# Attention 2: the bias of each exponential is made on GpSimd instead of VectorE

## The reference

```python
q = fq_sym((x @ Wq + bq) * scale, axis=-1)      # 16 heads of 16, 1024 queries
k = fq_sym(k, axis=-1);  v = fq_sym(v, axis=2)  # 1024 keys: all rows form one batch
attn = softmax(einsum('bhqd,bhkd->bhqk', q, k))
s = max(attn, axis=-1) / 255                    # fq_unsigned
attn = clip(round(attn / s), 0, 255) * s
out = einsum('bhqk,bhkd->bhqd', attn, v) @ Wp + bp
```

## Time and profile before

| | us |
|---|---|
| median of 3 runs | 1067.88 (1065.49 to 1070.03) |
| the profiled execution | 1065.92 |
| its span (first to last instruction) | 1064.3 |
| first to last start of the 128 exponentials | 315.65 to 511.08 |

### The profile page before, as it was taken

The page is one execution under the profiler, slowest core; times in us unless marked ns, Lnnn a source line. Parts: engine busy times, 40 slices in busy tenths (PEclk is TensorE's granted clock), DMA queues, the critical chain, the costliest instruction groups (busy, mean ns, idle before and its releaser), DMA issues.

```text
span 1064.3 us, 14257 instructions
## 1 busy us (share of the span) xinstructions
PE 720.2 (68%) x4990; PEld 484.0 (45%) x4990; DVE 544.2 (51%) x1256; ACT 387.1 (36%) x676; POOL 324.3 (30%) x338
## 2 busy tenths in 40 slices
PE   5964929930558787878776595294866239999980
PEld 3433514420435554555653484153435237677660
DVE  3995323246779988989344153727796200000002
ACT  3001113301269989999420132232653022202200
POOL 4720730058306766667205002400000320100005
PEclk9985969975668888888868697597898569999995
DMA  5060236638109989899502425430012130531503
GB/s 191 1 217 1 103 103 200 194 73 81 16 1 189 192 169 188 170 195 174 105 1 94 158 80 183 130 100 1 1 45 114 45 133 1 182 118 64 182 25 118
DMA packets 152028, 115.43 MB, mean 108 GB/s; under 512 B 108908, under 2 KB 138766, under 8 KB 150944
## 3 DMA queue, kind: packets, MB, share of 16 engines
q1 hardware_dynamic: 143256, 93.91, 34.2%
q0 software_dynamic: 7104, 19.42, 7.6%
q10 hardware_dynamic: 1608, 1.32, 0.4%
HBM read 63.98 MB, written 25.46 MB: 84 GB/s over the span
## 4 chain that ended last, share of the span: by engine, by line
PE 29%; DVE 9%; POOL 4%; issue 4%; DMA 4%; ACT 2%; POOLq 0%; DVEq 0%
PE psum L2030 8%; PE psum L2021 7%; PE psum L1394 3%; PE psum L187 2%; PE psum L1661 2%; POOL grouped_x_dram L1526 1%; POOL moe_x_dram L431 1%; PE psum L1409 1%; DMA both<-grouped_y_dram,idx 1%; PE psum L1251 1%; POOL both L474 1%; DVE both L1916 1%; DVE both L1913 1%; PE psum L527 1%; DVE stats L142 1%
## 5 line engine op out<-in xcount | busy, mean ns | idle before, releaser
L1200 DVE TENSOR_REDUCE both<-psum 128x1 f32<-128x1024 f32 x128 | 155.8, 1217 | 16.0 <-PE psum L1010 15.3
L929 POOL TENSOR_SCALAR both<-both 128x1024 f16<-128x1024 f32 x128 | 133.7, 1044 | 98.3 <-ACT both L1094 90.5
L1094 ACT ACTIVATE both<-psum,both 128x1024 f32<-128x1024 f32 x128 | 154.2, 1217 | 7.1 <-DVE both L1201 4.4
L431 POOL DMA_INDIRECT moe_x_dram<-xn,moe_idx_to x48 | 48.1, 1002 | 218.9 <-DVE moe_idx_from L419 204.9
L1010 PE MATMUL psum<-both 128*128 128x512 bf16 x256 | 92.6, 451 | 24.8 <-ACT both L1094 21.4
L2058 DVE COPY both<-psum 128x256 f32<-128x256 f32 (+1 forms) x24 | 10.1, 422 | 183.8 <-PE psum L2030 183.8
L2030 PE MATMUL psum<-both 128*128 128x256 f32 (+1 forms) x384 | 85.5, 381 | 0.0
L1031 PEld LDWEIGHTS psum<-both 128*128 128x128 f16 x1024 | 64.0, 100 | 46.9 <-ACT both L1101 14.7
L1031 PE MATMUL psum<-both 128*128 128x16 f16 x1024 | 69.8, 173 | 19.4 <-DVE xn L1208 8.1
L474 POOL DMA_INDIRECT both<-moe_y_dram,moe_idx_from x48 | 50.3, 1047 | 90.4 <-DMA moe_y_dram<-both 76.4
L2030 PEld LDWEIGHTS psum<-both 128*128 128x128 f32 (+1 forms) x384 | 65.2, 172 | 19.9 <-issue 4.2
(11 more groups left out here) (325 smaller groups left out, 1422.7 us busy)
## 6 DMA issues: line engine op xcount, KB each, us to landing
both<-in_l_experts SPq DMA_DIRECT2D x50, 384.0 KB, 3.9
both<-in_l_experts SPq DMA_DIRECT2D x8, 2048.0 KB, 8.8
grouped_y_dram<-both SPq DMA_DIRECT2D x31, 128.0 KB
grouped_x_dram<-zeros SPq DMA_DIRECT2D x15, 256.0 KB, 2.5
moe_x_dram<-zeros SPq DMA_DIRECT2D x1, 2560.0 KB, 9.1
both<-kpad_dram SPq DMA_DIRECT2D x1, 2048.0 KB, 8.1
both<-grouped_x_dram SPq DMA_DIRECT2D x1, 2048.0 KB, 13.1
both<-moe_x_dram SPq DMA_DIRECT2D x2, 1024.0 KB, 6.9
```

The lines of the kernel that those rows point to most:

```text
L431: nc.gpsimd.indirect_dma_start(out=self.x_dram[:, :], out_offset=bass.IndirectOffsetOnAxis(ap=self.idx_to[:, t, k:k + 1], axis=0), in_=xn[ ...
L929: nc.gpsimd.tensor_scalar(r2[n % RSLOTS2], e2[:, n % ESLOTS2, :], 1.0, HALF_BASE, ALU.mult, ALU.add).then_inc(sem("r2_ready"), 1)
L1094: nc.scalar.activation(e2[:, n % ESLOTS2, :], scores_at(n), ACT.Exp, bias=bias2[:, n:n + 1], scale=s2[:, t * H2 + h:t * H2 + h + 1], accum ...
L1200: seq.step(nc.vector.tensor_reduce(nmax2[:, n:n + 1], scores_at(n), AX.X, ALU.max, negate=True))
```

## The change

The bias step leaves DVE. DVE's maximum now signals a semaphore of its own, and POOL makes the bias from it. POOL's order becomes: bias 0, bias 1, rounding 0, bias 2, rounding 1, and so on to the end, so each bias step stands one unit ahead of the rounding of the unit before it.

```diff
         def l1x_rounds_gpsimd(pool):
-            for n in range(H2 * NT):
+            U = H2 * NT
+
+            def exp_bias(n):
+                h, t = n // NT, n % NT
+                pool.wait_ge(sem("nmax2_ready"), n + 1)
+                nc.gpsimd.tensor_scalar(bias2[:, n:n + 1], nmax2[:, n:n + 1], s2[:, t * H2 + h:t * H2 + h + 1], LN255,
+                                        ALU.mult, ALU.add).then_inc(sem("bias2_ready"), 1)
+
+            exp_bias(0)
+            for n in range(U):
+                if n + 1 < U:
+                    exp_bias(n + 1)
                 pool.wait_ge(sem("e2_ready"), n + 1)
                 if n:
                     pool.wait_ge(sem("r2_ready"), n)
@@ l1x_vector
             def top(n):
-                h, t = n // NT, n % NT
                 dve.wait_ge(sem("scores2_done"), n + 1)
-                seq.step(nc.vector.tensor_reduce(nmax2[:, n:n + 1], scores_at(n), AX.X, ALU.max, negate=True))
-                nc.vector.tensor_scalar(bias2[:, n:n + 1], nmax2[:, n:n + 1], s2[:, t * H2 + h:t * H2 + h + 1], LN255,
-                                        ALU.mult, ALU.add).then_inc(sem("bias2_ready"), 1)
+                nc.vector.tensor_reduce(nmax2[:, n:n + 1], scores_at(n), AX.X, ALU.max, negate=True).then_inc(sem("nmax2_ready"), 1)
```

## The result

The changed kernel took 1080.12 us (median of 4 runs, 1076.99 to 1081.90) against 1068.95 for the kernel before: 1.0094 times as long, 95% interval 1.0071 to 1.0117. It is slower by about 10 us (11.2 between the medians). The profiled execution took 1080.09, span 1078.5.

A forecast was written before the change was run, and what follows sets the result against it. In the second attention ACT is nearly full, with 7.1 us lost to DVE's pace and the score ring. 16 cycles at 6.02 and 9 at 6.08 give +3.2, boundaries -0.75: +2.4 us, 1070.3 as median; range 1063.5 to 1079.

The forecast's parts named there:

- rival B: Second attention: the small step on POOL is dear and POOL paces the stage; +9.9 us, 1077.8; chance 0.27.
- d: Last of each cycle's four exponentials a, b, c, d (a behind the copy); forecast to start 3.94 us behind a.
- DVE's pace: Second attention: reduce plus bias step take 1.38 us per unit on DVE; the change cuts this to about 1.25.
- score ring: Ring of three: unit d's scores wait for the end of a's exponential; counted in nine of 25 cycles.
- slow scores: Scores lasting 1.03 us with TensorE at 1.2 GHz; d at 4.00 behind a, nine cycles of 6.08 us.
- The loop through POOL's queue: bias(n+2) queues behind rounding(n), which needs exponential n: c at 2.70, d at 3.94 behind a, cycle 6.02 us.
- the rounding to the next POOL instruction: Link on POOL from a rounding's start to the next instruction's start, taken as 1.03 us.
- B: Duration of the bias step on POOL, taken as 0.22 us, bounds 0.11 and 0.41; counts twice in d's place.
- first link: From the start of exponential a to the start of a's rounding on POOL, taken as 1.41 us.
- The boundaries: Three group boundaries: reciprocal 0.13 us sooner and one gap about 0.12 shorter at each, 3 x -0.25 = -0.75 us.
- Rival C: Late roundings at the group boundaries starve PE: +4.5 us on top of the sum, 1074.8; chance 0.07.
- Rival A: Second attention: POOL is never late, only ACT's pace and the ring bind; -3.9 us, 1064.0; chance 0.13.

The follow-up runs named there:

- e1: Kernel before without any bias step, the exponential taking constant bias and scale columns: 0.9925 times the kernel before.
- e5: Against the changed kernel, POOL makes the bias only for units a and b, DVE for c and d: 0.9959 times the kernel before.
- e7: Against the changed kernel, POOL makes the bias only for units c and d, DVE for a and b: 1.0088 times the kernel before.
- e2: Kernel before, plus a like multiply-add on POOL ahead of each rounding that nobody waits for: 1.0042 times the kernel before.
- e8: Kernel before, plus a two-column add on POOL ahead of each rounding that nobody waits for: cycle 5.992 us against 5.915, one run.
- e4: Changed kernel with POOL's bias step two units ahead of its rounding instead of one: 1.0190 times the kernel before.

## Why the prediction was right in part, and where it was wrong

The measured +0.94%, put on the 1067.88 from which the prediction starts, is 1077.9 and lies in the range of 1063.5 to 1079, but I forecast +2.4 us and no measurable difference, at 0.59. What came is rival B, which I had at 0.27 and priced at +9.9 us; about +11 was measured in the medians and +12.0 in the stage. That the range held is luck in part: its upper end had d at 4.32 and cycles of 6.40, just what was measured (4.31, 6.40), but from a bias step of 0.41 that takes 0.264.

- **What bounds the kernel.** Right as to DVE's pace, which was what the change could win: without the bias step the time falls by 0.75% (e1). The share of the score ring was overrated. Of the nine cycles put down to d's slow scores, only two are of that kind (6.03 and 6.05, with a at 332.09 and 499.29, where d's maximum waited 0.4 us for its scores). In the other seven DVE waited 0.4 to 0.7 us for the scores of b, and c and d then came at DVE's pace of 1.38. One of them, with a at 349.49 and b at 350.68; the first line is b's maximum, the second c's, the last two are the exponentials c and d:

```profile
349.17 1.22 DVE L1200 TENSOR_REDUCE both<-psum 128x1 f32<-128x1024 f32 x1 [0.45 <-PE psum L1010]
350.56 1.22 DVE L1200 TENSOR_REDUCE both<-psum 128x1 f32<-128x1024 f32 x1
...
352.06 1.21 ACT L1094 ACTIVATE both<-psum,both 128x1024 f32<-128x1024 f32 x1
...
353.44 1.21 ACT L1094 ACTIVATE both<-psum,both 128x1024 f32<-128x1024 f32 x1
```

- **The loop through POOL's queue.** Right in its mechanism and its links: c and d wait for POOL in every cycle, a and b don't (b does in the first cycle and behind the boundaries), and e5 against e7 shows that the place in the cycle decides. It was sized too small.
- **The step that failed** is the term "the rounding to the next POOL instruction ... 1.03", taken from eight two-input operations in a row. Here it is 1.13, and from the bias step to the next rounding it is 0.35, not 0.21: behind each of them the next instruction starts 0.08 to 0.09 after the end, not before it. With B at 0.264 instead of 0.22, d's place is 1.40 + 1.13 + 0.35 + 1.13 + 0.30 = 4.31 instead of 3.94. Of these 0.37, 0.20 are the two spacings behind roundings, 0.09 twice B's error, and 0.10 the spacing behind the bias step, less 0.02 for the first link and the handover. 25 x 0.37 = 9.3 us, nearly the whole error of the sum.
- **Where B decides.** I set rival B's point at B = 0.29, on the condition that only B was unknown. B came at 0.264, under it, and the stage still went over: the spacings were a second unknown for which I had taken one row and no bound. The trace of before had such places outside the stage, which the prediction doesn't use. In one, POOL's second instruction waits for the first to be complete and starts 0.09 behind its end (677.89 less 676.76 + 1.04); the third starts 0.08 behind the second, and the trace shows no wait there:

```profile
676.76 1.04 POOL L1951 CAST both<-both 128x1024 f32<-128x1024 uint8 x1
677.89 1.10 POOL L1954 TENSOR_SCALAR both<-both 128x1024 f32<-128x1024 f32 x1
679.07 0.14 POOL L383 IOTA moe_code_base<- 128x8 f32 x1
```

- **The slow scores.** Forecast to lengthen nine cycles to 6.08. They don't show, though they are there (44 of the 128 pairs of score products took more than 0.85 us, 35 before): the loop through POOL at 6.40 is longer than the loop over the three score banks, which the prediction puts at 6.08.
- **The boundaries.** -0.75 forecast, -0.4 measured. Rival C didn't come: behind the boundaries PE waited for a transpose twice, 0.5 and 0.6 us, and over the stage its waits for DMA fell.
- **Rival A** would have needed the rounding to release POOL early. It didn't: in no undisturbed cycle did c stand less than 2.82 behind a.
- **POOL's load** was costed at nothing beside the loop. Alone it costs 0.42% (e2); by what way stays open, since e8 with slack has the same cycles. In the changed kernel it doesn't add to the loop, as each cycle is the sum of the loop's links already.
- **Slips in the sums.** The prediction gives +4.1 us for B = 0.265; by its own terms it is +4.3 (16 cycles at 6.11 and 9 at 6.125, less 0.75). For B = 0.15 it gives 1066.8 where its terms give 1067.6. Neither changes the forecast.

## What to carry to other kernels

When a small step goes to another engine, ask what it stands behind in that engine's queue and whether that work depends on the step's own consumer. If it does, a loop is made that pays the small step, the large one and every handover, however idle the engine looks: POOL was busy 71% of the undisturbed cycles before. Move the steps where the consumer's order already leaves a gap (here two of four, behind ACT's copy), and if an earlier place in the queue is tried, follow what its wait holds back, since in e4 the earlier place cost more than it saved.

## What the runs showed of the hardware that was not expected

- On POOL, the spacing of instructions isn't the duration: eight two-input products of 1.04 us came 1.03 apart, while a rounding of 1.04 has the next instruction 1.13 behind it, and a small one of 0.19 or 0.26 has it 0.27 or 0.35 behind, for a multiply-add (after, e2) and an add (e8) alike, and in e2 with no wait between a rounding and the step behind it. What makes the difference isn't settled.
- A scalar column on POOL costs 74 ns over an immediate (264 and 190 ns for one column); a two-input add of one column took 193 ns.
- POOL hands on to ACT in 0.03 to 0.04 us (396.16 + 0.264 to 396.46), no slower than DVE.
